# How far POOL's gathers may run ahead in the first layer of a two-layer graph kernel

## What is computed

```python
# layer 0: a softmax over the edges that enter a node, feature by feature
m = relu(feat[src]) + 1e-7
ex = exp(m - segment_max(m, dst)[dst])
a = ex / segment_sum(ex, dst)[dst]
x = layernorm(x + (feat + segment_sum(a * m, dst)) @ W + b)
# layer 1: attention with 8 heads over the same edges, edge features in the score
score = exp(clip(sum_head(K[src] * Q[dst] / sqrt(12) * E), -5, 5))
x = layernorm(x + segment_sum(V[src] * score, dst) / (segment_sum(score, dst) + 1e-6))
```

## Time and profile before

| | us |
|---|---|
| median of the runs | 4892.83 |
| the profiled execution, span | 4892.4 |
| PE busy | 3098.1 (63%) |
| POOL busy | 3143.9 (64%) |
| DVE busy | 2300.2 (47%) |
| ACT busy | 870.5 (18%) |
| first gather of layer one starts | 2.9 |
| last gather of layer one starts | 2383.5 |
| first gather of layer two starts | 2404.9 |

### The profile page before, as it was taken

The page is one execution under the profiler, slowest core; times in us unless marked ns, Lnnn a source line. Parts: engine busy times, 40 slices in busy tenths (PEclk is TensorE's granted clock), DMA queues, the critical chain, the costliest instruction groups (busy, mean ns, idle before and its releaser), DMA issues.

```text
span 4892.4 us, 43885 instructions
## 1 busy us (share of the span) xinstructions
PE 3098.1 (63%) x13152; PEld 2767.9 (57%) x13152; DVE 2300.2 (47%) x5605; ACT 870.5 (18%) x1966; POOL 3143.9 (64%) x3330
## 2 busy tenths in 40 slices
PE   3445444555555455455578777878777877877777
PEld 3344434444444444444477677767677777767676
DVE  5434344334433443344445555555555555555555
ACT  1222222222222222222201111111111111111111
POOL 6666666666666666666566666666666666666665
PEclk8666666666656667656665655565666565566665
DMA  3111111121111111111244444444444444444443
GB/s 97 40 40 43 42 39 40 40 45 40 40 44 41 39 40 45 40 39 40 67 111 111 114 112 114 112 111 117 112 111 111 114 112 114 112 114 110 115 113 98
DMA packets 290371, 383.51 MB, mean 78 GB/s; under 512 B 154382, under 2 KB 196911, under 8 KB 290127
## 3 DMA queue, kind: packets, MB, share of 16 engines
q0 software_dynamic: 132864, 251.83, 21.4%
q1 hardware_dynamic: 157263, 128.81, 9.5%
HBM read 360.62 MB, written 19.72 MB: 78 GB/s over the span
## 4 chain that ended last, share of the span: by engine, by line
POOL 31%; issue 23%; PE 18%; another core or an unknown queue 15%; DVE 9%; DMA 2%; ACT 2%; DVEq 0%; SPq 0%; ACTq 0%
POOL rows L454 31%; PE banks L605 4%; PE banks L586 4%; PE banks L577 4%; PE banks L547 3%; DVE onehot L817 2%; PE banks L596 2%; DMA rows<-in_x,src_i 1%; DVE sums L942 1%; DVE ex L930 1%; DMA rows<-key_value,src_i 1%; DVE banks L850 1%; ACT onehot_t L717 1%; DVE sums L940 1%
## 5 line engine op out<-in xcount | busy, mean ns | idle before, releaser
L454 POOL DMA_INDIRECT rows<-key_value,src_i x1661 | 1571.9, 946 | 922.2 <-issue 431.8
L454 POOL DMA_INDIRECT rows<-in_x,src_i x1661 | 1570.6, 946 | 811.6 <-issue 469.1
L547 PE MATMUL banks<-ex,onehot 128*128 128x192 f32 x3322 | 1036.0, 483 | 1026.7 <-DVE ex L930 810.5
L547 PEld LDWEIGHTS banks<-ex,onehot 128*128 128x128 f32 x3322 | 865.2, 288 | 1188.8 <-DVE ex L930 933.9
L586 PE MATMUL banks<-qw,onehot_t 128*128 128x192 f32 x1664 | 609.2, 515 | 401.2 <-ACT onehot_t L717 233.1
L605 PEld LDWEIGHTS banks<-onehot,vals 128*104 128x104 f32 x3322 | 601.2, 272 | 260.2 <-issue 210.3
L605 PE MATMUL banks<-onehot,vals 128*104 128x64 f32 x3322 | 608.2, 359 | 183.8 <-issue 151.5
L586 PEld LDWEIGHTS banks<-qw,onehot_t 128*128 128x128 f32 x1664 | 440.3, 302 | 449.1 <-ACT onehot_t L717 258.4
L577 PE MATMUL banks<-we_sb,ea 97*128 97x96 f32 x3322 | 672.1, 372 | 0.0
L577 PEld LDWEIGHTS banks<-we_sb,ea 97*128 97x128 f32 x3322 | 662.2, 295 | 0.0
L930 DVE SCALAR_TENSOR_TENSOR ex<-banks,ex 128x384 f32<-128x384 f32 x416 | 229.0, 550 | 795.7 <-issue 654.5
(11 more groups left out here) (107 smaller groups left out, 1480.4 us busy)
## 6 DMA issues: line engine op xcount, KB each, us to landing
ea<-in_edge_t SPq DMA_DIRECT2D x415, 192.0 KB
rows<-in_x,src_i POOLq DMA_INDIRECT x1661
rows<-key_value,src_i POOLq DMA_INDIRECT x1661
qw<-query SPq DMA_DIRECT2D x832, 24.0 KB
key_value<-qkv SPq DMA_DIRECT2D x24, 400.0 KB
x<-in_x SPq DMA_DIRECT2D x7, 672.0 KB, 8.2
query<-qkv SPq DMA_DIRECT2D x24, 192.0 KB
out<-outs SPq DMA_DIRECT2D x24, 192.0 KB
```

What stands on the lines that cost most here:

```text
L454: pool.indirect_dma_start(out=to[0:n, r, u, :], out_offset=None, in_=table, in_offset=bass.IndirectOffsetOnAxis(ap=src_i[0:n, g * G + u:g ...
L547: last = nc.tensor.matmul(ps_sum0[b], onehot[:, r, u, :], ex[:, b, u, :], start=u == 0, stop=u == n - 1)
```

## The change

A constant PACE0 = 5 is added, and the first layer's wait uses it in place of PACE = 3: ahead of the first gather of group g, POOL now asks for min(g - 5, 2(g - 8)) + 1 sums. The second layer keeps PACE.

```diff
 QA = 3
+PACE0 = 5
 PACE = 3
...
                 for g in range(R0, NG):
-                    pool.wait_ge(s_sum, min(g - PACE, 2 * (g - R0)) + 1)
+                    pool.wait_ge(s_sum, min(g - PACE0, 2 * (g - R0)) + 1)
                     gather(g, g % R0, xr, x, s_row[g % R0])
```

## The result

The changed kernel takes 4905.05 us (median, 4900.57 to 4910.50) against 4892.25 us of the kernel before in the same comparison (4889.77 to 4894.48), eight runs each. The ratio is 1.0026 with a 95% interval of 1.0017 to 1.0034: slower by 13 us, where 60 us of gain were forecast. The time lies in the range of 4640 to 4920, on the wrong side of no change.

A forecast was written before the change was run, and what follows sets the result against it. POOL's gathers bound layer one, each 1.25 us of work plus 0.18 us of stall waiting for PE's held words. The profiled 4892.4 - 64 + 4 gave 4832; against the median, 4893 - 60 = 4833 us, range 4640 to 4920.

The forecast's parts named there:

- The hold goes with running gathers: Layer one: PE's word of a finished sum is held, 7.4 us for group 41, while POOL's gathers run.
- the hold sets in at the same place, and POOL gets two groups further: 28 gathers a cycle in place of 20: Layer one's new steady cycle: 28 gathers, then a 4.34 us pause, 1.394 us a gather in place of 1.433.
- The term of -64 us: Layer one's gathers: 0.039 us saved on each of 1625 by less pause per gather.
- The row I leaned on: Layer one's start: 36 gathers, then a 4.75 us pause, against 3.93 after 20; used to size the new pause.
- slower rival: Layer one: the toll grows faster than the run of gathers, +73 us, 4966 us; chance 0.22.
- the pause is paid per gather: Rival for layer one: pauses are proportional to gathers, 1.433 us each stays, pauses only regroup, 4895 us; chance 0.22.
- The leftover: Layer one's end: up to two more groups run through ACT, DVE and PE after the last gather, +4 us.
- If the hold waits for the pause, it lasts those 10 us longer too: Layer one: with five groups of lead POOL gathers 10 us more before standing, and the hold lengthens by as much.
- The 17 us "in a piece": Sign in the profile after: DVE's addition held some 17 us in a piece, where it was 5 to 9.
- A sum in the rivals: Rival that stalls are absorbed: 4596 us, or about 4710 with half the holds ending so; chance 0.18 in whole or mostly.
- The Trainium skill: Warning that dense semaphore increments from one engine can block another; read as supporting the slower case, 4966 us.
- Layer two: Second layer keeps its pace, waits and work: 0 change, within a few us of its 2487.

The follow-up runs named there:

- the staged kernel: Changed kernel with eight ways of feeding layer one in sequence (leads, fillers, plain DMAs, 64-row gathers); 4666.41 us where the kernel before took 4907.32.
- the other run: The same change run again against the kernel before, in a later batch where before took 4892.64 us; 4903.91 us, ratio 1.0025.

## Why the prediction was wrong

- **What bounds the kernel** was read right: POOL's gathers with 0.18 us of stall each, paid because PE's word of a finished sum is held while gathers run. "The hold goes with running gathers" stands: in the staged kernel words were late where POOL's own pace was 1.200 to 1.336 us a gather, and on time at 1.495 us and with plain DMAs. The late word does not come from the matmuls alone either: the same matmuls, fed by plain DMAs in the same trace, never made DVE wait for over 1.4 us, and in the traces without held words the word comes within 0.02 us of their recorded end. The prediction took the hold for a fixed trait of the kernel, though; it is one of some batches.
- **The step that failed** is "the hold sets in at the same place, and POOL gets two groups further: 28 gathers a cycle in place of 20", with a pause of 4.34 us. No run of 28 came. POOL paused 129 times (I had said 58), mostly behind runs of 16 and 4, the longest after the start 24, with pauses of about 4.5 us. The pause is no price of a cycle but a debt of each gather: 1.43 less 1.25 us. The term of -64 us was 5.6 us of loss in the one run and 2.0 in the other.
- **The row I leaned on** was one: after 36 gathers at the start POOL paused 4.75 us, 0.8 more than after 20, and I drew a line through the two. But the layer begins without any earlier debt, and those 36 gathers were followed by more pauses, as the 1.478 us of the first 72 in my own slower rival showed. The evidence against the line, "the rate is the same in every part of the layer", stood in the text under a rival with a chance of 0.22. A rate that does not change over 2300 us while single pauses run from 0.5 to 4 us was the stronger row.
- **The rival "the pause is paid per gather"** had the mechanism: 1.433 kept, pauses only regrouped, 4895. It missed by 10 us because of the next point.
- **The leftover** was sized at 4 us, two groups of 2.1 us. It is 9.5 us, 13.2 in the other run. The last word is released with POOL's last gather, and then a whole node stage with the last groups, 16.2 us, stands behind it; before, 9.4 of 16.4 us of the same work ran beside gathers. The 2.1 us of a catch-up leave the node stage out.
- **"If the hold waits for the pause, it lasts those 10 us longer too"** came true: the longest hold, from the end of the matmuls to DVE's addition, went from 9.8 to 19.4 us. The 17 us "in a piece" were right as the length of a hold. DVE's idle time in a piece is shorter, 12.2 us at the longest and 9.4 before, because DVE has other work in the meantime. So the error was not in the hold but in its price: I let a longer hold cost hardly more than a short one.
- **A sum in the rivals**: with half of the 301 us saved the time is 4893 - 150 + 4 = 4747, not 4710. It moves neither the forecast nor the answer.
- **Slower** had the right sign with the wrong reason: the toll does not grow with the run at five groups. At eight it does a little. The stated range of 4640 to 4920 holds the measured time, but the forecast's mechanism does not reach it: that is luck.
- **The Trainium skill** (VectorE: DVE Perf Modes, the section on the TRN2 errata) advises to space increments that come on completion. The page speaks of a deadlock, and nothing here stood for good, so what I made of it, a longer block from denser increments, was a guess beyond the page. In the staged kernel spacing the gathers to 1.495 us does end the holds and is still a loss, since the spacing costs more than the holds did, 1.496 against 1.429 us a gather; spaced to 1.336 us they still cost 1.434. Whether those increments are the cause no run shows.
- **Layer two** kept its work: 2.7 us less, within the few us allowed.

## What to carry to other kernels

When a producer is held back at an even rate, work out the time per item over the whole stage before reading single pauses: if it is the same everywhere, as here, expect a longer lead to regroup the pauses, to leave their sum, and to add a longer leftover after the last item. Measure a late word from the end of the work that it tells of, and not by the idle time of the engine that waits; and see whether a shorter lead waits for the same thing, before the two are put in one row. Run the kernel before in several batches ahead of explaining a stall; here 700 of 4893 us belonged to the batch. And where only some batches show an effect, put the ways to be compared in one kernel, one behind the other, and look at what stands at the borders of the stages.

## What the runs showed of the hardware that was not expected

- The kernel before takes 4892 to 4910 us in three batches and the first comparison's, and 4192 to 4194 us in the others. Both layers change, by the traces of the kernels beside it too: the first from 1.433 us a gather at a lead of three to 1.248 at any lead from three on, the second's gathers from 2474 us to 2077. What makes a batch the one or the other is open. It is not the program, and not the chip alone: one chip had both. The mean granted clock of these runs was 0.62 to 0.64 with held words and 0.67 to 0.69 without; whether that is cause or effect no run shows.
- With held words, indirect gathers get through at one per 1.43 us at best, and PE's words stay away while POOL is faster, for up to 9.8 us from the matmuls' end to DVE's addition at a lead of three and 19.4 us at five. A gather of 64 rows costs the same as one of 128 then, and without held words 1.200 against 1.248 us: nearly all of the price is per gather.
- A lead of two or of eight groups costs 1.452 and 1.454 us a gather, where three and five cost 1.433 to 1.436. At two POOL mostly waits for the sums themselves. Why eight is worse stays open.
- Plain DMAs of the same bytes in place of the first layer's gathers end the layer's bound: 3229 us in place of 4192 without held words, and in the staged kernel 0.63 us a tile from POOL with held words, with no late word beside it.
